# Squares of the turned probabilities laid out block by block, and the first transferred group sent in two halves

## What is computed

```python
y = ((xg - mu) * jax.lax.rsqrt(var + EPS)).reshape(B, C, H, W)
y = y * gn_gamma[None, :, None, None] + gn_beta[None, :, None, None]
qkv = jnp.einsum('bchw,dc->bdhw', y, w_qkv) + b_qkv[None, :, None, None]
q, k, v = jnp.split(qkv, 3, axis=1)
...
scores = jnp.einsum('bnc,bcm->bnm', q, k) * C ** (-0.5)
w = jax.nn.softmax(scores, axis=-1)
a = jnp.einsum('bnm,bmc->bnc', w, v)
...
out = jnp.einsum('bchw,dc->bdhw', a, w_out) + b_out[None, :, None, None]
return x + out
```

## Time and profile before

| | |
|---|---|
| median of 3 runs | 137.25 us (136.85 to 137.44) |
| the profiled execution: its own time | 138.07 us |
| its span, first to last instruction | 136.3 us |
| PE busy | 129.4 us (95%) |
| DVE busy | 99.8 us (73%) |
| ACT busy | 65.0 us (48%) |
| POOL busy | 41.4 us (30%) |
| DMA issues of swaps | 2 x 48, of 128 KB |

### The profile page before, as it was taken

How to read it: one execution, slowest core, us unless ns; L and a number is a source line. 1 busy time by engine, 2 the same in 40 slices (tenths; PEclk the granted TensorE clock), 3 DMA queues, 4 the chain that set the end, 5 groups by cost and what they waited for, 6 DMA issues and landing times.

```text
span 136.3 us, 1759 instructions
## 1 busy us (share of the span) xinstructions
PE 129.4 (95%) x543; PEld 89.1 (65%) x543; DVE 99.8 (73%) x170; ACT 65.0 (48%) x117; POOL 41.4 (30%) x49
## 2 busy tenths in 40 slices
PE   6999999998999949999999999999999999999990
PEld 6987688875777526666666666666656577554670
DVE  0589699999998996877686889866868886761302
ACT  3154778854675372544542475544633474730000
POOL 6032130730022229300190058000770367303210
PEclk9999999999999999999999999999999999999999
DMA  4940000030056978985689656888888459961011
GB/s 152 350 191 0 0 5 0 3 77 0 0 111 147 210 188 236 207 203 169 154 204 206 204 114 160 191 195 224 203 202 201 122 123 209 209 176 77 0 77 77
DMA packets 8937, 19.01 MB, mean 139 GB/s; under 512 B 3040, under 2 KB 3040, under 8 KB 8928
## 3 DMA queue, kind: packets, MB, share of 16 engines
q1 hardware_dynamic: 8640, 18.63, 53.8%
q10 hardware_dynamic: 288, 0.27, 0.6%
HBM read 4.20 MB, written 2.11 MB: 46 GB/s over the span
## 4 chain that ended last, share of the span: by engine, by line
PE 75%; DVE 12%; SPq 7%; issue 2%; DMA 2%; DVEq 0%
PE mixed L833 31%; PE scores L778 7%; SPq L255 7%; PE scores L779 7%; PE scores L781 7%; DVE scores L577 5%; PE scores L839 4%; PE turned L798 3%; DVE flipped_odd L605 3%; PE turned L723 3%; DMA home_odd<-flipped_odd 2%; PE mixed L830 1%; PE mixed L828 1%; PE mixed L829 1%; PE mixed L723 1%
## 5 line engine op out<-in xcount | busy, mean ns | idle before, releaser
L577 DVE TENSOR_SCALAR_CACHE_REDUCE scores<-scores,key_bias 128x1024 f32<-128x1024 f32 x31 | 40.0, 1289 | 15.0 <-PE scores L781 14.7
L426 ACT ACTIVATE probs<-scores,neg_max 128x1024 f32<-128x1024 f32 x32 | 35.7, 1116 | 22.7 <-DVE scores L577 21.9
L833 PE MATMUL mixed<-home_odd,v 128*128 128x512 f32 x48 | 22.6, 594 | 1.9 <-DMA home_odd<-flipped_odd 1.9
L833 PE MATMUL mixed<-home_even,v 128*128 128x512 f32 x48 | 22.1, 594 | 0.0
L778 PE MATMUL scores<-y_hi_odd,z_hi_odd 128*128 128x512 f32 x32 | 18.7, 585 | 0.6 <-DVE z_lo_odd L544 0.6
L778 PE MATMUL scores<-y_hi_even,z_hi_even 128*128 128x512 f32 x30 | 15.9, 531 | 0.0
L605 DVE STREAM_TRANSPOSE flipped_odd<-probs 128x1024 f32<-128x1024 f32 x12 | 14.8, 1235 | 0.3 <-DMA home_odd<-flipped_odd 0.3
L605 DVE STREAM_TRANSPOSE flipped_even<-probs 128x1024 f32<-128x1024 f32 x12 | 14.8, 1234 | 0.0
L833 PEld LDWEIGHTS mixed<-home_even,v 128*128 128x128 f32 x48 | 8.9, 189 | 7.8 <-issue 7.2
L833 PEld LDWEIGHTS mixed<-home_odd,v 128*128 128x128 f32 x48 | 8.5, 190 | 8.3 <-issue 8.0
L779 PE MATMUL scores<-y_lo_odd,z_hi_odd 128*128 128x512 f32 x32 | 12.6, 392 | 0.0
(11 more groups left out here) (162 smaller groups left out, 202.9 us busy)
## 6 DMA issues: line engine op xcount, KB each, us to landing
home_odd<-flipped_odd SPq DMA_DIRECT2D x48, 128.0 KB, 2.4
home_even<-flipped_even SPq DMA_DIRECT2D x48, 128.0 KB, 2.4
out_dram<-result SPq DMA_DIRECT2D x8, 256.0 KB, 3.5
inv_wide<-inverse_rows SPq DMA_DIRECT2D x7, 256.0 KB, 3.6
xs<-in_x_dram SPq DMA_DIRECT2D x2, 512.0 KB, 6.5
xs<-in_x_dram SPq DMA_DIRECT2D x3, 256.0 KB, 4.6
xs<-in_x_dram ACTq DMA_DIRECT2D x1, 256.0 KB, 3.3
ws<-in_weights_dram SPq DMA_DIRECT2D x1, 256.0 KB, 4.0
```

The lines of the kernel that those rows point to most:

```text
L426: act.activation(probs[:, i % RING, :], scores[:, i % 2, :], ACT.Exp, bias=neg_max[:, i:i + 1], scale=-1.0, accum_out=row_sum[:, i:i + 1]) ...
L577: dve.tensor_scalar(scores[:, i % 2, :], scores[:, i % 2, :], key_bias[:, b % 2, i:i + 1], None, ALU.subtract, ALU.min, accum_out=neg_max[ ...
L833: mm = pe.matmul(bank, v[:, b % 2, k, :], there, start=first, stop=final)
```

## The change

The order of the values in flipped and home becomes band, block, key tile, column in place of band, key tile, block, column. So a band of a single block is one run of 256 values (1 KB), and two blocks are one run of 2 KB. flip writes by the new order, and mix reads by it. swap takes a range of blocks lo to hi: it waits for the flips up to hi and moves those blocks' part of every band. For group 1, SP's queue gets swap(1, 0, 2), keep_rows(1), swap(1, 2, 4) in place of keep_rows(1), swap(1): 32 DMAs of 32 rows of 2 KB in place of 16 of 32 rows of 4 KB. The other five groups are moved as before. The counts that are waited for (swaps) grow by 16 DMAs for the odd groups.

```diff
--- before.py
+++ after.py
@@ -41,6 +41,7 @@
     VW = C + 2
     SQ = 4
     GROUP = QB * N
+    SQUARES = 32 * KT
     GROUPS_OF_FOUR = BATCHES * HALVES
     SWAPPED = range(1, 7)
     LAST = GROUPS_OF_FOUR - 1
@@ -212,9 +213,13 @@
 
             return n if n < QB else n - QB * len(SWAPPED)
 
+        def swap_parts(group):
+
+            return 2 if group == SWAPPED[0] else 1
+
         def swaps(group):
 
-            return SWAP * len([g for g in SWAPPED if g <= group and g % 2 == group % 2])
+            return sum(SWAP * swap_parts(g) for g in SWAPPED if g <= group and g % 2 == group % 2)
 
         def copy_of_turned(to, n, j):
 
@@ -245,15 +250,15 @@
                 sp.dma_start(inv_wide[:, group % 2, :],
                              inverse_rows[group].partition_broadcast(128)).then_inc(s_wide[group % 2], 16)
 
-            def swap(group):
-                sp.wait_ge(s_flipped, QB * group)
+            def swap(group, lo, hi):
+                sp.wait_ge(s_flipped, QB * (group - 1) + hi)
                 if group > 2:
                     sp.wait_ge(s_mixed, KT * (group - 1))
                 for k in range(SQ):
                     for g in (0, 2, 1, 3):
                         t = g ^ k
-                        sp.dma_start(home[group % 2][32 * t:32 * t + 32, g * N:(g + 1) * N],
-                                     flipped[group % 2][32 * g:32 * g + 32, t * N:(t + 1) * N]
+                        sp.dma_start(home[group % 2][32 * t:32 * t + 32, g * N + lo * SQUARES:g * N + hi * SQUARES],
+                                     flipped[group % 2][32 * g:32 * g + 32, t * N + lo * SQUARES:t * N + hi * SQUARES]
                                      ).then_inc(s_swapped[group % 2], 16)
 
             def store(group):
@@ -267,8 +272,13 @@
             keep_rows(0)
             spread_rows(0)
             for group in SWAPPED:
-                keep_rows(group)
-                swap(group)
+                if group == SWAPPED[0]:
+                    swap(group, 0, 2)
+                    keep_rows(group)
+                    swap(group, 2, QB)
+                else:
+                    keep_rows(group)
+                    swap(group, 0, QB)
                 spread_rows(group)
                 if group >= 2:
                     store(group - 2)
@@ -602,7 +612,7 @@
                 dve.wait_ge(s_exp, n + 1)
                 if group > 2:
                     dve.wait_ge(s_swapped[group % 2], swaps(group - 2))
-                dve.transpose(flipped[group % 2][:, :].rearrange("p (tv u c) -> p tv u c", u=QB, c=32)[:, :, u, :],
+                dve.transpose(flipped[group % 2][:, :].rearrange("p (t u v c) -> p u t v c", t=SQ, u=QB, c=32)[:, u, :, :, :],
                               probs[:, n % RING, :].rearrange("p (v t r) -> p t v r", t=SQ, r=32)
                               ).then_inc(s_flipped, 1)
 
@@ -829,7 +839,7 @@
                         pe.matmul(bank, v_hi[:, k, :], last_tail[:, k, :], start=False, stop=False)
                         mm = pe.matmul(bank, v_lo[:, k, :], last_head[:, k, :], start=False, stop=final)
                     else:
-                        there = home[g][:, :].rearrange("p (g v u c) -> p v u g c", g=SQ, v=KT, u=QB)[:, k, :, :, :]
+                        there = home[g][:, :].rearrange("p (g u v c) -> p v u g c", g=SQ, u=QB, v=KT)[:, k, :, :, :]
                         mm = pe.matmul(bank, v[:, b % 2, k, :], there, start=first, stop=final)
                     mm.then_inc(s_mixed, 1)
                 tiles_mixed[group] += count
```

## The result

The changed kernel takes 144.45 us (median of 4 runs, 143.71 to 144.84) against 137.34 us before: a ratio of 1.0514, 95% interval 1.0461 to 1.0568. It is 7.1 us slower; 6.9 were forecast. The profiled execution took 144.5 us, with a span of 142.7 us against 136.3.

A forecast was written before the change was run, and what follows sets the result against it. PE was taken as the bound, without a pause from 51 us on. From a median of 137.25 us, 5.0 for the later landing and 1.9 for the clock gave 144.1 us, range 139.8 to 146.0.

The forecast's parts named there:

- PE without slack behind 51 us: PE is busy throughout 51.00 to 127.40 us, so any delay at 51 us arrives undiminished at the end.
- The layout at nothing: Flips and mix matmuls in the new order: no cost expected, bounds 0.05 us per flip and 0.2 us for mixing.
- The early start, 5.65 us: Group 1's first half needs only flips 4 and 5; its first DMA goes at 32.30 in place of 37.95.
- 0.635 us for the issue of half a DMA: On SP's queue, a 64 KB swap DMA keeps the 128 KB pitch; the bounds considered were 0.555 and 0.32.
- Rival B: Group 1's swap: data set the pitch, half DMAs take 0.32 us, the pause vanishes, 135.4 us; chance 0.14.
- The landing: Group 1's last DMA lands at 55.85 in place of 50.86, 4.99 us later; PE's pause grows to 6.84 us.
- The slow issue: One of group 1's issues on SP takes 1.04 us more than its neighbours; expected as the group's fourth.
- The clock: PE's pause ahead of mix(1) most likely ends at 1.2 GHz, costing 1.9 us, between 0 and 2.5.
- The sum: Whole kernel: 5.0 us of later landing plus 1.9 of clock make 6.9, giving 144.1 us.
- Nothing else late: Behind group 1, spread_rows(1) and group 2's swap still arrive before their readers, which move later too.

The follow-up runs named there:

- e1: Kernel before with only the new order of the squares, group 1 still in 16 DMAs of 128 KB behind its fourth flip: 137.61 us, ratio 1.0021.
- e2: Changed kernel, but the first half also waits for the fourth flip, 32 DMAs of 64 KB behind keep_rows(1): 149.57 us, ratio 1.0914.
- e4: Kernel before with the last four of group 1's sixteen DMAs issued from ACT's queue, SP issuing twelve: 137.44 us, ratio 1.0000.
- e8: Kernel before with group 1's sixteen DMAs replaced by four of 128 partitions and 512 KB, squares not exchanged: 136.07 us, ratio 0.9896.
- e5: Changed kernel with 24 matmuls of zeros ahead of PE's wait for group 1's squares: 142.04 us, ratio 1.0339.
- e9: Kernel before with four 512 KB DMAs a group, each from 32 source partitions to 128, the flip reading each fourth key: 146.7 us, ratio 1.0599.
- e7: Changed kernel with group 1's tiles mixed at steps 12 to 14 in place of 11 to 14: 142.52 us, ratio 1.0251.

## Why the prediction was right

*PE without slack behind 51 us, so the shift reaches the end.* Right: 7.0 us read in the stretch, 7.1 in the medians.

*The layout at nothing.* Right: e1 gives 1.0021, the flips 1.240 us.

*The early start, 5.65 us.* Right: flip 5 ends and SP issues at 31.88, with the whole stretch 0.4 earlier; e2 without the early start is 5.1 us slower, keep_rows' price included.

*0.635 us for the issue of half a DMA.* Right, and the term that decides: 10.08 us for sixteen, 0.634 each in e2. Rival B (the engines set the pitch) is excluded for half squares by the same rows, with the engines busy at 0.37. The prediction's argument against B was too wide, though. It took SP to be the only limit; e4 shows that for whole squares more issues brought only a sixth more than SP's pace (240 to 206 GB/s). B was no rival here because with half squares SP asked for no more than 91 GB/s.

The Trainium skill's "SBUF — State Buffer" ("Door 1: The DMA port swizzle") has 32 partitions reach half of the ports, with some 218 GB/s at most. The runs agree in the direction: 397 GB/s with 128 partitions at either end in e8, 240 with squares of 32 in e4. The figure they don't bear out for such squares, as 240 is above it; in e4 squares of different bands were under way at once, and no run has a single band alone.

*The landing.* Forecast: 23.55 us behind the first issue. Measured: 55.16 - 31.88 = 23.28. Half a DMA lands in 2.02 us, 0.32 sooner, and keep_rows took 0.58 in place of 0.44. The pause was 6.57 for 6.84. The slow issue came, as counted, but in the second half and not in the first. That it came at all was not assured: among e2's 32 issues there is none, and without it the shift would have been about 1 us less.

*The clock.* Right in kind, and e5 isolates it: 2.3 to 2.4 us. The term was set at 1.9, between 0 and 2.5. Its upper bound came from the start, where 20 matmuls follow each other at 0.232 us; the prediction took that pace for the lower level, but the granted clock of that stretch (1.04 to 5.68 us, kernel before) reads 1.00. So no row of the kernel before showed the price, and that 4.56 us at the lower level came near the 5 taken is partly luck. The row of the end had the clock fall after 2.98 us without work; here it took 4.3, in e9 it fell 0.7 us after PE had gone back to work from a pause of 2.8, and in e7 it did not fall in every execution, so one row was no safe guide to the moment.

*The sum.* 5.0 + 1.9 for 4.7 + 2.3: both terms were off by 0.3 to 0.4 us, in opposite directions. That the forecast is so close (144.1 for 144.45) is partly the luck of this.

*Nothing else late.* Right: SP issued group 2's swap from 54.89 to 64.9, and PE never waited for home_even.

Open: what makes an issue of 32 partitions cost 0.59 us where the small ones take 0.32; why one issue in thirty or so takes 1.5 us and more; and how much of e4's longer landings is the engines' limit and how much the two queues' getting in each other's way.

## What to carry to other kernels

Before a transfer is split to start its first part early, count the issues and not the bytes: the early start buys (time gained) / (pitch) issues, here 5.65 / 0.635 = 9, and the split cost 16. As each of the sixteen squares needs the last block too, sixteen issues stay behind the last flip on a single queue. At a pitch that half the bytes don't shorten, the split could have landed sooner by no more than the 0.3 us of the shorter landing. A wait on the engine that bounds the kernel is to be priced with its clock: a pause of 6.6 us cost 2.3 more in the 4.6 us behind it.

## What was not expected of the hardware

- The issue of a square doesn't depend on its bytes: 0.59 us for 32 rows of 2 KB and of 4 KB alike. That is no rule for all issues: four of 512 KB from 32 partitions took from 0.59 to 4.34 us (e9), four of 512 KB from 128 partitions 0.57 to 1.22 (e8).
- With two queues issuing squares at once landings lengthened from 2.4 to as much as 4.9 us, and an issue of SP's from 0.59 to 0.92, at 240 GB/s (e4), though 128-partition DMAs reach 397 (e8).
- Behind a wait of no more than 2.77 us the granted clock fell to 0.50 (e9).
- A read with a step of 16 bytes doubles PE's distance from matmul to matmul (0.23 to 0.46 us, fp32r, 128x512) and makes a DVE transpose of 128x1024 fp32 take 2.03 us for 1.24. Runs of 128 bytes cost neither of them anything that shows: four mix matmuls take 1.88 us from them as from one run, and a flip takes 1.24 us whether it writes runs of 128 bytes or of 1 KB (e1).
